# A graph network's GRU cell on one core: the three steps of the blend move from VectorE and GpSimd to GpSimd alone

## The reference

```python
def _gru_cell(x, h, W_ih, W_hh, b_ih, b_hh):
    gi = x @ W_ih.T + b_ih
    gh = h @ W_hh.T + b_hh
    ...
    r = jax.nn.sigmoid(i_r + h_r)
    z = jax.nn.sigmoid(i_z + h_z)
    n = jnp.tanh(i_n + r * h_n)
    return (1.0 - z) * n + z * h
...
h = jnp.maximum(_layernorm(x, axis=-1), 0.0)
x = x + _L0_gnn_ref(h, edge_index, edge_type_9, 12500, ...)
```

## Time and profile before

| what | value |
|---|---|
| median of three runs | 6133.05 us (6127.13 to 6144.72) |
| the profiled execution: its own time, its span | 6150.87 us, 6148.8 us |
| GpSimd, VectorE, ScalarE, TensorE matmul busy, whole span | 3592.3, 2171.7, 2000.3, 3286.6 us |
| L588, the blend's sum on GpSimd | 49 of them |
| L1181 and L1187, difference and product on VectorE | 49 of each |
| mean granted TensorE clock over the span | 0.642 of full speed |

### The profile page before, as it was taken

How to read it: one execution, slowest core, us unless ns; L and a number is a source line. 1 busy time by engine, 2 the same in 40 slices (tenths; PEclk the granted TensorE clock), 3 DMA queues, 4 the chain that set the end, 5 groups by cost and what they waited for, 6 DMA issues and landing times.

```text
span 6148.8 us, 85445 instructions
## 1 busy us (share of the span) xinstructions
PE 3286.6 (53%) x19136; PEld 2671.0 (43%) x19137; DVE 2171.7 (35%) x4141; ACT 2000.3 (33%) x4208; POOL 3592.3 (58%) x3971
## 2 busy tenths in 40 slices
PE   4555556666666666667733333333433333337776
PEld 4444445445544544546532333222323323237775
DVE  8444444444444444445600000000000000027774
ACT  5222222222222222223522222221222212238886
POOL 2555556566665665663266666666666666666651
PEclk8555556665666556658755555555555555569999
DMA  4222211111111111111222222222212222236664
GB/s 141 57 58 56 55 52 42 41 42 42 43 43 40 43 43 40 43 43 53 65 72 71 73 71 71 72 71 69 74 68 75 71 69 74 69 114 224 221 221 142
DMA packets 251756, 466.50 MB, mean 76 GB/s; under 512 B 66550, under 2 KB 169129, under 8 KB 237581
## 3 DMA queue, kind: packets, MB, share of 16 engines
q0 software_dynamic: 106944, 226.05, 12.4%
q1 hardware_dynamic: 144717, 239.48, 11.9%
HBM read 315.00 MB, written 150.28 MB: 76 GB/s over the span
## 4 chain that ended last, share of the span: by engine, by line
another core or an unknown queue 34%; issue 24%; PE 23%; ACT 7%; SPq 6%; DVE 3%; ACTq 1%; DMA 1%; POOL 1%; DVEq 0%; POOLq 0%
PE ps L1563 7%; PE ps L1535 6%; PE ps L1410 4%; PE ps L1424 3%; ACT sb_counts L702 2%; SPq L405 2%; ACT ps L709 2%; SPq L406 2%; SPq L407 1%; PE ps L1432 1%; ACT sb_ring L788 1%; ACTq L784 1%; SPq L416 1%; DVE sb_oh L1237 1%
## 5 line engine op out<-in xcount | busy, mean ns | idle before, releaser
L573 POOL DMA_INDIRECT sb_ring<-msg_table,sb_idxslot x1664 | 1581.1, 950 | 1098.0 <-SPq L418 619.5
L603 POOL DMA_INDIRECT rows_by_src<-sb_ring,sb_idxslot x1664 | 1617.0, 972 | 864.4 <-issue 503.3
L1535 PE MATMUL ps<-sb_H,sb_oh 128*128 x3520 | 865.5, 414 | 1540.9 <-issue 1130.9
L1535 PEld LDWEIGHTS ps<-sb_H,sb_oh 128*128 128x128 f32 x3520 | 724.8, 299 | 1681.7 <-issue 1678.7
L1410 PE MATMUL ps<-sb_ring,sb_oh 128*128 x3520 | 849.2, 415 | 328.6 <-SPq L414 172.7
L1237 DVE TENSOR_SCALAR sb_oh<-sb_oh,sb_cf 128x512 f32<-128x512 bf16 x440 | 206.4, 492 | 2188.2 <-remote 1425.1
L1410 PEld LDWEIGHTS ps<-sb_ring,sb_oh 128*128 128x128 f32 x3520 | 734.7, 305 | 398.9 <-issue 392.2
L702 ACT CAST sb_counts<-ps 54x512 bf16<-54x512 f32 x440 | 254.4, 578 | 1919.0 <-remote 1030.5
L788 ACT COPY sb_ring<-ps 128x512 f32<-128x512 f32 x416 | 242.1, 582 | 1791.8 <-remote 1290.9
L1123 DVE TENSOR_TENSOR sb_Y<-sb_Y,ps 128x512 f32 x440 | 300.6, 683 | 746.8 <-remote 485.9
L1563 PE MATMUL ps<-sb_oh,sb_H 128*128 128x128 f32 x3520 | 432.6, 281 | 163.0 <-issue 116.8
(11 more groups left out here) (216 smaller groups left out, 3571.6 us busy)
## 6 DMA issues: line engine op xcount, KB each, us to landing
sb_H<-rows_by_src SPq DMA_DIRECT2D x110, 1088.0 KB, 5.0
sb_oh<-step_targets SPq DMA_DIRECT2D x110, 512.0 KB
sb_ring<-msg_table,sb_idxslot POOLq DMA_INDIRECT x1664
rows_by_src<-sb_ring,sb_idxslot POOLq DMA_INDIRECT x1664
rows_by_src<-sb_cf SPq DMA_DIRECT2D x198, 68.0 KB
msg_table<-sb_oh SPq DMA_DIRECT2D x14, 448.0 KB, 3.2
sb_oh<-in_x SPq DMA_DIRECT2D x49, 128.0 KB, 2.1
x_after_layer<-sb_H SPq DMA_DIRECT2D x49, 128.0 KB, 1.9
```

The source lines that it names most:

```text
L573: pool.indirect_dma_start(out=ring[:, r * G + q, 0:F], out_offset=None, in_=table_d[:, :], in_offset=bass.IndirectOffsetOnAxis(ap=idxslot[ ...
L603: pool.indirect_dma_start(out=rows_d[:, :], out_offset=bass.IndirectOffsetOnAxis(ap=idxslot[:, h, g * G + q:g * G + q + 1], axis=0), in_=r ...
L1535: m = mm(picked_ps[:, ds(slot, P)], pick[g][:, q * P:(q + 1) * P], H[:, ds(off, P)], start=False, stop=True, skip_group_check=True)
```

## The change

The difference and the product leave `cell_turn` on VectorE and go to `cell_n` on GpSimd, ahead of the sum that is there already. GpSimd now waits for the tanh (`cand`) and for its own difference (`cell_h`) and product (`zhn_ready`). Turns 0 and 1 of its loop are written out ahead of the loop. On VectorE the wait for `cand` of the turn before goes with the difference.

```diff
             def cell_n(i, k):
+                pool.wait_ge(S("cand"), i + 1)
+                wait(pool, "hn_ps", i - 1)
+                nc.gpsimd.tensor_tensor(hnbuf[k], H[:, ds(i * GW, GW)], nbuf[k], ALU.subtract).then_inc(S("cell_h"), 1)
+                pool.wait_ge(S("cell_h"), i + 1)
+                nc.gpsimd.tensor_tensor(hnbuf[k], hnbuf[k], zbuf[k], ALU.mult).then_inc(S("zhn_ready"), 1)
                 pool.wait_ge(S("zhn_ready"), i + 1)
                 nc.gpsimd.tensor_tensor(hnbuf[k], hnbuf[k], nbuf[k], ALU.add).then_inc(S("hn_ready"), 1)
 
-            with pool.Fori(0, (TURNS - 1) // 2) as j:
+            for k in range(2):
+                cell_n(k, k)
+            with pool.Fori(1, (TURNS - 1) // 2) as j:
                 for k in range(2):
                     cell_n(j * 2 + k, k)
             cell_n(TURNS - 1, 0)
...
-                gate, blend, add = last < TURNS, first >= 1 and last - 1 < TURNS, first >= 2 and last - 2 < TURNS
+                gate, add = last < TURNS, first >= 2 and last - 2 < TURNS
...
-                if blend:
-                    dve.wait_ge(S("cand"), i)
-                    wait(dve, "hn_ps", i - 2)
-                    vs.tensor_tensor(hnbuf[o], H[:, ds((i - 1) * GW, GW)], nbuf[o], ALU.subtract).then_inc(S("cell_h"), 1)
                 if gate:
                     dve.wait_ge(S("cell_t"), i + 1)
                     vs.tensor_tensor(tbuf[k], tbuf[k], bank(2 * k + 1)[:, 0:GW], ALU.add).then_inc(S("cand_in"), 1)
-                if blend:
-                    dve.wait_ge(S("cell_h"), i)
-                    vs.tensor_tensor(hnbuf[o], hnbuf[o], zbuf[o], ALU.mult).then_inc(S("zhn_ready"), 1)
```

## The result

Over 12 executions of each kernel on the same chip the median went from 6128.18 us (6121.95 to 6144.72) to **6144.82 us** (6126.48 to 6159.01). The ratio is 1.0025, with a 95% interval of 1.0015 to 1.0036: 9 to 22 us more. That is slower. The ratio itself is within the 0.3% that the forecast called no change, its interval reaches a little past it. The forecast was 6145 us, which was +12.0 us on the 6133.05 of three executions. Over 12 executions the kernel before came out 4.9 us lower than that and the difference of the medians is 16.6 us.

The account below looks back on a forecast made before the run. A closed chain per pair of turns was taken to bound the cell: 0.49 at the start + 23 pairs x 0.46 + 0.97 at the end = +12.0 us on 6133.05, taken as 6145 us, range about 6130 to 6164.

Parts of the forecast that it names:

- What bounds it: Cell stage: a closed chain through the blend sets each pair of turns at 6.76 us; additions are paid once per pair.
- The wake-up from the tanh: From the tanh's end to the difference on GpSimd: taken as 0.24 us, ends 0.03 and 0.31.
- A hand-over of GpSimd to itself: Between difference, product and sum on GpSimd: taken as 0.08 us, as L588 woke after VectorE's product.
- the slower rival: GpSimd's waits on itself, about 52, cost more than 0.08 us: 6156 us at 0.30, 6181 at 0.78; chance 0.22.
- A step: One blend operation on GpSimd, shaped like L588: priced at 0.726 us.
- The step "from the tanh's end at 2999.77": Cell's end: six GpSimd steps without a pause, 4.92 us to 3004.69 against 3003.72, so +0.97 us.
- The start: Turn 0, from the tanh's end to `back`: 2.48 us against 1.99, so +0.49 us.
- What VectorE's relief is worth: Removing 41.3 us of differences and products from VectorE gains nothing, as that work is not on the chain.
- a sign of being right: Among the signs in the changed kernel's profile: VectorE down by 41 us, GpSimd up by 71.
- The port: Rival: VectorE's copy L1172 blocks GpSimd's next step by up to 0.17 us per pair, 6149 us; chance 0.10.
- Its cover: If VectorE's copy waits up to 0.73 us for GpSimd, L1184's 1.9 us of slack covers it.
- The clock: Rival: TensorE's granted clock falls; at half the clock, +113 us more; held nearly excluded, chance 0.03.

Follow-up runs that it names:

- a fourth step: Kernel after the change plus a GpSimd addition of a tile of zeros at the blend's end: pair 8.03 us, stretch 191.2 us, against 7.23 and 171.6.
- tanh first: Kernel after the change with the tanh put ahead of the message copy in ScalarE's loop: pair 6.95 us, stretch 165.5 us, against 7.23 and 171.6.
- order only: Kernel before the change with VectorE's addition L1184 put behind the product: pair 6.55 us, stretch 155.8 us, against 6.76 and 160.0.
- both orders: Kernel before the change with L1184 behind the product on VectorE and the tanh ahead of the message copy on ScalarE: pair 6.28 us, ratio 0.9983.
- both inputs in SBUF: Kernel after the change plus two spare VectorE additions per turn, both inputs in SBUF: pair 7.35 us, stretch 174.6 us, against 7.23 and 171.6.
- the blend in one row: Kernel before the change with difference, product and sum in a row on VectorE, then L1184: pair 6.67 us, stretch 159.1 us, against 6.76 and 160.0.
- spare additions from PSUM: Kernel after the change plus two spare VectorE additions per turn, one input in PSUM: pair 7.23 us, stretch 171.6 us, stage 190.3 us.

## Why the prediction was right

**What bounds it**: right. The chain of a pair was read at 6.76 us. The runs moved it by 0.14 (only the product), 0.47 (the change), 0.80 (a fourth step, against after), -0.28 (tanh first, against after), -0.21 (order only) and -0.48 us (both orders), each within 0.04 of what was put on or taken off it, on three different engines. That is shown. The sum failed in two places: with both inputs in SBUF, where the hold-up was priced too high, and with the blend in one row, where VectorE itself became the bound.

**The prices.** The wake-up from the tanh was taken as 0.24 and is 0.26. A hand-over of GpSimd to itself was taken as 0.08 and is 0.08; this was the value on which the slower rival hung. That rival's 0.30 and 0.78 came from DMAs. The row nearest in kind, not the only row of a self-wait, was the right one. A step was taken as 0.726 and is 0.724 to 0.729. The pair was to grow by 0.46 and grew by 0.47.

**The sum.** +12.0 forecast, 12.0 measured in the stage, but two terms were off in opposite ways. From turn 0's `back` to turn 46's:

```profile
2842.73 0.44 PE L1495 MATMUL ps<-sb_cf,sb_oh 128*128 128x128 f32 x2 [0.99 <-POOL sb_oh L593]
2849.97 0.44 PE L1495 MATMUL ps<-sb_cf,sb_oh 128*128 128x128 f32 x2 [0.96 <-POOL sb_oh L593]
...
3009.05 0.44 PE L1495 MATMUL ps<-sb_cf,sb_oh 128*128 128x128 f32 x2 [1.17 <-POOL sb_oh L593]
...
3014.00 0.69 PE L1495 MATMUL ps<-sb_cf,sb_oh 128*128 128x128 f32 x2 [1.60 <-POOL sb_oh L593]
```

That is 166.3 us against 155.2, so +11.1 where 23 x 0.46 = 10.6 was forecast. The first pair grew by more, 0.68: before, it was only 6.56 us, and VectorE's written-out difference woke 0.20 faster. Behind turn 46 the end grew by 0.36, not 0.97: from 3009.05 to 3014.00, 4.95, against 2999.19 to 3003.78, 4.59. The step "from the tanh's end at 2999.77" counted the last GpSimd steps from a tanh of the other turn of the pair. That tanh ended 0.58 us behind the start of turn 46's `back` before and 0.11 behind it after, so 0.47 of the growth of the pairs was counted twice. The start was forecast at +0.49 and is +0.48 (tanh's start 2839.73 to `back` 2842.73, 3.00 us, against 2841.47 to 2843.99, 2.52).

**What VectorE's relief is worth**: nothing, as forecast, shown by putting it back. Its size was misjudged: a sign of being right was to be VectorE down by 41 us, and it went down by 23.0 over the span. The moved instructions last 0.42 us, but the next one starts 0.34 behind them, so they held VectorE for only about 98 x 0.34 = 33 us, and the copies took 8.4 us more (49 of them, 16.7 us in place of 8.35). GpSimd went up by 74.9 us where 71 was forecast.

**The port.** The forecast gave little to it, since the one meeting in the trace of before showed no block. The block does happen: the copy ran 0.47 us at 2928.20 and ended with GpSimd's step L591. Its cover held, as the forecast said: VectorE has time. The fear that it would hold GpSimd up fell with the run without the copy. The weakness was in the evidence: one meeting of two short instructions was too little to lean on, and only the slack made it harmless.

**The clock**: right, 1.00 in the cell of both profiled executions. **The range and chances**: the median fell 0.2 us from the forecast, which is luck within a scatter of 33 us over 12 executions: the base was 4.9 us too high and the step 4.6 too low. By its own working the low end of the range should have been 6136 - 9 = 6127, not 6130, which changed nothing; the interval of the ratio, 9 to 22 us, also reaches past the 18.4 us that were drawn as the border to slower. Why the centre of that interval is some 3 us over the stage's 12 stays open. The profiled executions show no change of length behind the cell that goes beyond their scatter: from the stage's end to layer 1's sum it is 2489.2 us before and 2480.3 after, where nine of the twelve traces span 2477.6 to 2489.2 and the three on the chip where both orders were timed 2495.1 to 2505.0.

## What to carry to other kernels

Find the closed chain first: follow one result from engine to engine until it comes back to where it started, and see after how many turns it does. A step moved to another engine is priced by its latency on that chain, its wake-up included, and once per round of the chain; the busy share of the engine it leaves says nothing, as long as that engine is not the bound itself, as VectorE was with the whole blend. And look at the order on every queue that the chain passes: two swaps of lines, on VectorE and ScalarE, gave 0.17%, where moving work to an idle engine had cost 0.25%.

## What the runs showed that was not expected

- The lock between VectorE and GpSimd was uneven: VectorE's instruction with two SBUF inputs went from 410 to 878 ns, GpSimd's beside it from 729 to 785.
- A copy of four elements per partition on VectorE took up to 619 ns beside GpSimd, where it had taken 172 at most. Held-up copies ended 0.02 to 0.03 us after a GpSimd step, held-up additions of 128 x 256 0.28 us after it.
- On VectorE two dependent instructions of 128 x 256 start 0.45 us apart, independent ones 0.34. With the whole blend on VectorE, filling one gap was worth 0.25 us per pair (6.42 against 6.67).
- TensorE's granted clock in the first 7 us of the cell was 1.00 in five traces and 0.53 to 0.57 in seven, of kernels with the same code up to there (but for one memset on VectorE in the kernel without the copy). In the 20 us before TensorE had been busy 14.0 to 17.4 us in the five and 14.7 to 17.5 in the seven. It made the way to the first `back` 2.6 to 2.9 us longer (13.3 and 13.5 us in the kernels with spare additions from PSUM and without the copy, against 10.7 in after).
